# A decay product in bf16 over three exact terms, with dummy products ahead of the heads, in an three-phase gated block on one core

## What is computed

```python
def _mlstm_head(q, k, v, ig, fg, eps=1e-06):
    log_f = jax.nn.log_sigmoid(fg)
    cs = jnp.concatenate([zeros, jnp.cumsum(log_f, axis=0)], axis=0)
    log_d = jnp.where(jnp.tri(s, dtype=bool), (cs - cs.T)[1:, 1:] + ig.T, neg)
    m = jnp.max(log_d, axis=-1, keepdims=True)
    d = jnp.exp(log_d - m)
    c = q @ (k.T / jnp.sqrt(dh)) * d
    n = jnp.maximum(jnp.sum(c, axis=-1, keepdims=True), jnp.exp(-m))
    return c / (n + eps) @ v
...
gate_in = jnp.concatenate((q, k, v), axis=-1)      # q = layernorm(x), k = v = ctx
ig = gate_in @ igate_kernel + igate_bias
fg = gate_in @ fgate_kernel + fgate_bias
```

## Time and profile before

| | us |
|---|---|
| runs | 608.34, 601.44, 603.51; median 603.51 |
| profiled execution: time | 601.67 |
| profiled execution: span from first to last instruction | 599.9 |
| TensorE busy | 474.9 (79%) |
| VectorE busy | 346.9 (58%) |
| ScalarE busy | 306.2 (51%) |
| GpSimd busy | 237.9 (40%) |
| granted TensorE clock, mean | 0.859 |

### The profile page before, as it was taken

One profiled execution on the slowest core, in us unless ns is written; L12 is line 12 of the kernel. 1 busy time (PEld: TensorE's weight loads), 2 busy tenths in 40 slices (PEclk: granted clock), 3 DMA queues, 4 the chain that ended last, 5 costly groups with the idle time before them and its releaser, 6 DMA issues. The chain is left out here.

```text
span 599.9 us, 12767 instructions
## 1 busy us (share of the span) xinstructions
PE 474.9 (79%) x3771; PEld 352.3 (59%) x3771; DVE 346.9 (58%) x1447; ACT 306.2 (51%) x764; POOL 237.9 (40%) x226
## 2 busy tenths in 40 slices
PE   0349999999999999974459999999607777777774
PEld 0337677877787778663327777777504445455552
DVE  6223588687878777787312333332214787788873
ACT  1346576666666656422113333333215677777873
POOL 5200114444444444466500000000088888888810
PEclk9998788677777767895569999999955999999998
DMA  5981112222222211140122343333143556555521
GB/s 139 184 162 55 54 55 75 70 68 75 67 76 68 73 52 50 43 124 27 36 62 54 105 106 105 105 106 89 52 101 45 111 120 136 120 108 128 134 72 52
DMA packets 85067, 51.98 MB, mean 87 GB/s; under 512 B 7555, under 2 KB 78886, under 8 KB 85030
## 3 DMA queue, kind: packets, MB, share of 16 engines
q1 hardware_dynamic: 73766, 43.09, 27.0%
q0 software_dynamic: 11264, 8.43, 8.2%
HBM read 26.07 MB, written 16.91 MB: 72 GB/s over the span
## 5 line engine op out<-in xcount | busy, mean ns | idle before, releaser
L665 POOL DMA_INDIRECT s_xs<-slots_y,s_gidx x64 | 98.9, 1545 | 152.3 <-DMA slots_y<-s_ye 134.7
L803 ACT ACTIVATE s_ht<-heads,s_cols 128x512 f32<-128x512 f32 x64 | 44.0, 687 | 85.1 <-PE heads L1044 84.8
L147 ACT ACTIVATE s_xn<-s_xs,s_ln_shift,s_ln_rstd 128x128 f32 (+1 forms) x192 | 77.6, 481 | 17.2 <-DVE s_ln_shift L140 16.8
L99 DVE BATCH_NORM_STATS2 s_ln_stats<-s_xs 128x6 f32 (+1 forms) x256 | 55.0, 280 | 35.2 <-DMA s_xs<-slots_y,s_gidx 19.2
L643 POOL DMA_INDIRECT slots_x<-s_xn,s_sidx x64 | 62.8, 982 | 22.9 <-issue 22.9
L629 POOL TENSOR_TENSOR s_hs<-s_hs,s_head_w 128x512 f32<-128x512 f32 x16 | 20.3, 1268 | 109.0 <-DVE s_hs L1268 108.9
L1044 PE MATMUL heads<-s_xet,s_w_sb 128*128 128x512 f32 x128 | 59.8, 612 | 1.7 <-DVE s_xet L1384 1.7
L1051 PE MATMUL bank<-s_w_sb,s_ht 128*128 128x128 f32 x512 | 59.9, 276 | 0.9 <-DVE s_ye L1393 0.9
L1051 PEld LDWEIGHTS bank<-s_w_sb,s_ht 128*128 128x128 f32 x512 | 58.5, 192 | 1.5 <-issue 1.5
L943 PE MATMUL heads<-s_dec_r,s_dec_l 128*128 128x512 f32 x64 | 50.6, 938 | 0.0
L968 PE MATMUL heads<-s_vaug,s_cw 64*64 64x33 f32 x1024 | 47.4, 261 | 0.3 <-DVE s_cw L1230 0.3
(11 more groups left out here) (181 smaller groups left out, 962.0 us busy)
## 6 DMA issues: line engine op xcount, KB each, us to landing
slots_x<-s_xe SPq DMA_DIRECT2D x8, 516.0 KB, 11.4
s_xe<-slots_x SPq DMA_DIRECT2D x16, 258.0 KB, 3.2
s_xs<-in_x_dram SPq DMA_DIRECT2D x16, 256.0 KB, 2.9
s_ctxb<-in_ctx_dram SPq DMA_DIRECT2D x16, 256.0 KB, 3.1
s_kpt<-s_kt SPq DMA_DIRECT2D x16, 256.0 KB, 2.4
s_w_sb<-in_L_ffn_w_dram SPq DMA_DIRECT2D x16, 256.0 KB
slots_y<-s_ye SPq DMA_DIRECT2D x16, 256.0 KB, 2.3
s_ctxv<-in_ctx_dram SPq DMA_DIRECT2D x16, 256.0 KB
```

Of the source, the lines that this page charges most:

```text
L99: last = dve.bn_stats(self.stats[:, i * GT + t, :], tile(t))
L147: last = act.activation(out(t), tile(t), ACT.Identity, bias=self.shift[:, j:j + 1], scale=self.rstd[:, j:j + 1])
L665: pool.indirect_dma_start(out=xs[:, n * D:(n + 1) * D], out_offset=None, in_=slots_y, in_offset=bass.IndirectOffsetOnAxis(ap=gidx[:, n:n + ...
L803: act.activation(ht[:, s_par, c, :], heads[:, c, :], ACT.Gelu_apprx_tanh, bias=col).then_inc(h_done, 1)
```

## The change

An fp32 value is split into three terms. Its upper half-word, read as bf16, is the first term; what is left after subtracting it is an fp32 value again, whose upper half-word is the second term, and once more for the third. The three sum to the value. `top_half` reads every second half-word of an fp32 tile as bf16, so that no term is written as bf16 anywhere.

`am` gets 48 columns (three groups of 16) and `mrow` three rows of 128 for each pair. VectorE computes the differences: two more steps after `am` and two after the scan, each waiting for the one before. `turn_a` transposes 48 columns, the copy to `dec_l` takes 48 rows, six DMAs in place of two bring the maxima to rows 48 to 53 of `dec_r`, and SP's two waits ahead of them change places. The two products of `decay_exponents` read the upper halves of both operands. On GpSimd the constants are written for the new rows (`CONSTS` 30 to 34). And TensorE's `first_pass` calls `keep_clock(1, 4)` after `gate_products`: four dummy products of 512 columns to bank 1.

```diff
+def top_half(ap):
+    return ap.bitcast(BF16).rearrange("p (n w) -> p n w", w=2)[:, :, 1]
...
-        am = sb("am", [P, 2, R])
-        mrow = sb("mrow", [R, 2, P])
+        am = sb("am", [P, 2, 3 * R])
+        mrow = sb("mrow", [R, 2, 3, P])
+        pick = sb("pick", [3 * R, 2, R])
...
             def spread_max(g, half, q):
+                hold(sp, l_ps, g - 1, consts)
                 hold(sp, mrow_done, g + 1, consts)
-                hold(sp, l_ps, g - 1, consts)
-                for b in range(2):
-                    sp.dma_start(dec_r[32 + b:33 + b, q, :], mrow[:, q, b * S:(b + 1) * S]).then_inc(m_in[q], 16)
+                for j in range(3):
+                    if j:
+                        hold(sp, m_terms, nth(g, j, 2), consts)
+                    for b in range(2):
+                        row = 3 * R + 3 * b + j
+                        sp.dma_start(dec_r[row:row + 1, q, :], mrow[:, q, j, b * S:(b + 1) * S]).then_inc(m_in[q], 16)
...
             def turn_a(g, half, q):
-                pe.wait_ge(a_done, g + 1)
-                pe.transpose(bank[6][0:R, 128:256], am[:, q, :], ident[:, :]).then_inc(at_ps, 1)
+                hold(pe, a_terms, nth(g, 2, 2), consts)
+                pe.transpose(bank[6][0:3 * R, 128:256], am[:, q, :], ident[:, :]).then_inc(at_ps, 1)
...
             def decay_exponents(g, half, q):
                 pe.wait_ge(arow_done, g + 1)
-                hold(pe, m_in[q], half * 32 + 32, consts)
+                hold(pe, m_in[q], half * 96 + 96, consts)
                 need(pe, cw_done, nth(g - 1, 2, 2))
                 for u in range(2):
-                    last = pe.matmul(heads[:, u, :], dec_l[:, q, :], dec_r[:, q, u * GW:(u + 1) * GW], start=True, stop=True)
+                    last = pe.matmul(heads[:, u, :], top_half(dec_l[:, q, :]), top_half(dec_r[:, q, u * GW:(u + 1) * GW]),
+                                     start=True, stop=True)
...
                 if one:
                     gate_products(*one)
+                    keep_clock(1, 4)
                 if three:
                     head_values(*three)
...
             def a_values(g, half, q):
-                dve.tensor_tensor(am[:, q, :], gates[:, 0, :], bank[6][:, 64:64 + R], ALU.subtract).then_inc(a_done, 1)
+                dve.tensor_tensor(am[:, q, 0:R], gates[:, 0, :], bank[6][:, 64:64 + R], ALU.subtract).then_inc(a_done, 1)
+                dve.wait_ge(a_done, g + 1)
+                for j in range(2):
+                    if j:
+                        dve.wait_ge(a_terms, nth(g, 1, 2))
+                    term = am[:, q, j * R:(j + 1) * R]
+                    dve.tensor_tensor(am[:, q, (j + 1) * R:(j + 2) * R], term, top_half(term), ALU.subtract).then_inc(a_terms, 1)
...
             def running_max(g, half, q):
-                dve.tensor_copy(dec_l[0:R, q, :], bank[6][0:R, 128:256]).then_inc(arow_done, 1)
+                dve.tensor_copy(dec_l[0:3 * R, q, :], bank[6][0:3 * R, 128:256]).then_inc(arow_done, 1)
...
-                dve.tensor_tensor_scan(mrow[:, q, :], reset[:, :], bank[6][0:R, 128:256], 0.0, ALU.add, ALU.max).then_inc(mrow_done, 1)
+                dve.tensor_tensor_scan(mrow[:, q, 0, :], reset[:, :], bank[6][0:R, 128:256], 0.0, ALU.add, ALU.max).then_inc(mrow_done, 1)
+                dve.wait_ge(mrow_done, g + 1)
+                for j in range(2):
+                    if j:
+                        dve.wait_ge(m_terms, nth(g, 1, 2))
+                    term = mrow[:, q, j, :]
+                    dve.tensor_tensor(mrow[:, q, j + 1, :], term, top_half(term), ALU.subtract).then_inc(m_terms, 1)
```

More of the change, by code:

```diff
@@ L338, in flamingo @@
         a_done = sem("a_done")
+        a_terms = sem("a_terms")
+        m_terms = sem("m_terms")
         at_ps = sem("at_ps")
@@ L429, in one_row @@
             return v.rearrange("(a n) -> a n", a=1)
-        CONSTS = 30
+        CONSTS = 34
         block = ctx.enter_context(nc.Block())
@@ L598, in _ @@
             pool.wait_ge(cleared, 4)
[L599 to L602, removed]
+            step(pool.memset(pick[:, :, :], 0.0))
+            for j in range(3):
+                step(pool.affine_select(out=pick[:, :, :], in_=pick[:, :, :], compare_op=ALU.not_equal, fill=1.0, base=-j * R,
+                                        pattern=[[0, 2], [-1, R]], channel_multiplier=1))
+            step(pool.tensor_copy(dec_r[0:3 * R, :, :].rearrange("p q (r i) -> p (q r) i", i=S),
+                                  pick[:, :, :].rearrange("p q r -> p (q r)").unsqueeze(2).to_broadcast([3 * R, 2 * R, S])))
             step(pool.tensor_copy(dec_r[S:P, :, :].rearrange("p q (r i) -> p (q r) i", i=S),
@@ L606, in _ @@
                                   ident[S:P, S:P].unsqueeze(1).to_broadcast([S, 4, S])))
[L607 to L611, removed]
+            step(pool.memset(dec_l[32:S, :, :], -1.0))
+            for b in range(2):
+                half = dec_l[32:S, :, b * S:(b + 1) * S]
+                step(pool.affine_select(out=half, in_=half, compare_op=ALU.is_ge, fill=0.0, base=32 - 3 * R - 3 * b,
+                                        pattern=[[0, 2], [0, S]], channel_multiplier=1))
+                step(pool.affine_select(out=half, in_=half, compare_op=ALU.is_ge, fill=0.0, base=3 * R + 3 * b + 2 - 32,
+                                        pattern=[[0, 2], [0, S]], channel_multiplier=-1))
             step(pool.memset(reset[:, :], 0.0))
@@ L1219, in running_max @@
                 need(dve, l_ps, g - 1)
-                dve.tensor_copy(dec_l[0:R, q, :], bank[6][0:R, 128:256]).then_inc(arow_done, 1)
+                dve.tensor_copy(dec_l[0:3 * R, q, :], bank[6][0:3 * R, 128:256]).then_inc(arow_done, 1)
                 if not isinstance(g, int) or g >= 2:
-                    dve.wait_ge(m_in[q], half * 32)
-                dve.tensor_tensor_scan(mrow[:, q, :], reset[:, :], bank[6][0:R, 128:256], 0.0, ALU.add, ALU.max).then_inc(mrow_done, 1)
+                    dve.wait_ge(m_in[q], half * 96)
+                dve.tensor_tensor_scan(mrow[:, q, 0, :], reset[:, :], bank[6][0:R, 128:256], 0.0, ALU.add, ALU.max).then_inc(mrow_done, 1)
[5 more added lines that the diff above has]
+                    dve.tensor_tensor(mrow[:, q, j + 1, :], term, top_half(term), ALU.subtract).then_inc(m_terms, 1)
             def decayed_scores(g, q, u):
```

2 lines of the change are left out of this document (1 added, 1 removed).

## The result

| | before | after |
|---|---|---|
| median of the runs, us | 604.46 (601.44 to 608.34, 4 runs) | 620.07 (617.61 to 629.66, 4 runs) |
| ratio, 95% interval | | 1.0241 [1.0149, 1.0333] |
| profiled execution, time and span, us | 601.67, 599.9 | 617.61, 615.9 |
| granted clock over the span | 0.859 | 0.805 |

The time is inside the range of the prediction (591 to 628), but not where its forecast put it (606, within 1% of before). What came is the first rival, the clock that comes back only with the scores, for which the prediction gave 0.30 and 625 us. The interval of the ratio is clear of 1, but not of 2%.

What follows compares the result with a forecast made beforehand. The first phase was taken as bound by a loop through VectorE and TensorE, with TensorE's clock; -1.0, +1.0 and +0.35 us a pass made +4.6 over 13 passes, less 2 at the ends: 606 us, range 591 to 628.

Steps and rivals of the forecast that it cites:

- the first rival: TensorE's clock comes back only with the scores: 2.4 us a pass in 9 of 13, 625 us, chance 0.30.
- stretch A: From `s_am` to the one-hot in each pass, 4.30 us, taken to belong to VectorE.
- stretch B: From the one-hot to the next `s_am`, 10.41 us, taken to belong to TensorE, with VectorE waiting 1.59 us at its end.
- (1): Decay product on TensorE as two bf16 products: 0.60 us high, about 1.0 low, saving 2.3 a pass.
- (2): Four dummies ahead of the heads on TensorE: 0.86 us high, 1.7 low, 1.3 in the mean, on the path.
- (3): Four more VectorE steps between `s_am` and the one-hot: 0.42 and 0.62 us, taken as +1.0 a pass.
- (4): `turn_a` on TensorE waits for the second term and turns 48 columns instead of 16: nothing, at most 0.1 us.
- (5): Six row transfers on SP instead of two: 3.5 us of issue, hidden with 2.6 us to spare.
- (6): GpSimd's setup changes by four steps, swallowed by VectorE's later 6.78 us wait for a transfer of `s_xs`: 0.
- The late terms: Rival: the decay product waits for the sixth row, half a microsecond late, +0.5 a pass, 612 us, chance 0.07.
- (7): TensorE's clock stays low over turns and logits in about one pass of three: +0.35 us a pass.
- the ends of the phase: Three first passes and one last of the first phase, where B alone counts: 4 x -0.5 = -2 us.

Runs made afterwards that it cites:

- e2: The kernel before with only the four dummy products added between gates and heads: 626.16 us, ratio 1.0338 to the kernel before.
- e10: The changed kernel with only the first term and 17 dummies spread over the pass in place of four: 587.26 us, ratio 0.9727 to the kernel before.
- e9: The changed kernel with all three terms and 17 dummies spread over the pass in place of four: 595.26 us, ratio 0.9862 to the kernel before.
- e7: The kernel before with only the four VectorE steps added, their results unused: 625.47 us, ratio 1.0218 to the kernel before.
- e6: The changed kernel without dummies and with only the first term, so no added VectorE steps: 604.66 us beside 606.61 of the kernel before.
- e1: The changed kernel without its four dummy products: 612.04 us, ratio 1.0109 to the kernel before.
- e4: The changed kernel with 13 dummies spread over token count, gates and heads in place of four: 604.32 us, ratio 0.9920 to the kernel before.
- e5: The kernel before, with fp32 product and no added VectorE steps, given 13 spread dummies: 610.92 us beside 606.61 of the kernel before.
- e8: The changed kernel with 13 spread dummies and the two `s_mrow` steps on GpSimd instead of VectorE: 630.27 us, ratio 1.0340 to the kernel before.

## Why the prediction was right in its range and wrong in its forecast

The frame held: one loop, stretch A with VectorE, stretch B with TensorE, and the clock over both. Of the seven steps:

- **(1) The product**: right. 1.06 us low and 0.61 high for the two, taken as 1.0 and 0.60. The strided operands cost nothing that shows, so the upper bound of 1.88 is out.
- **(2) The dummies**: the size was off. 1.3 us was a mean of both levels, the runs show 1.55 a group in after and 1.75 in e2, since the level falls just there. "Net of (1) and (2) on B: -1.0" would have been -0.6.
- **(3) The four steps**: their length was right (0.38 and 0.59 against 0.42 and 0.62; A grew from 4.5 to 5.3 in the mean from the 7th to the 14th pass, and by 1.0 from e10 to e9). By the formula of the Trainium skill (VectorE: DVE Perf Modes, section on the TRN2 errata) one such `s_mrow` step is estimated at 0.29 us, and the trace has 0.59 for two. Wrong was that they cost just their length. In the long passes of after they are hidden: the one-hot is done at 169.3 us and TensorE's scores at 170.8, and TensorE waits for the one-hot for 1.0 us in all of the steady part. In e7, with the fp32 product, they cost 1.7 a pass. The step took A and B as separate terms, and what a longer A costs depends on when TensorE comes to the one-hot, and at which level it goes on.
- **(4), (5), (6)**: right. L959 is in no pass behind `s_dec_r`; its idle time is 0.2 us of its own issue. Six issues took 3.79 us (3.5 predicted), landing 1.8. The late terms are out. On setup, the wait of the earlier trace rows became 5.56 us at 37.76, 1.4 us sooner.
- **(7) The clock**: this is the step that failed. It took +0.35 a pass, the low level over turns and logits in one pass of three. Measured per group are +0.79 on the turns, +0.52 on the logits, +0.91 on the scores and +0.58 on the heads, 2.8 together. With the product (-2.1), the dummies (+1.55) and the gates (-0.25) this is +2.0 of busy time, which overlaps at its edges, for passes 1.5 longer. Scores ran low in 9 of 16 groups, and the first rival had "9 of 13" passes at 2.4 us; what happened is 7 of ten steady passes at 2.3 over the mean of before (17.30 less 15.04), and three between 0.7 under it and 0.6 over.

Some of the agreement is luck. For the ends of the phase the sum had -2, at half of B's -1.0 a pass and without a reason for the half. The two end stretches gave -3.4 and +1.4. Two readings were off without harm: A from +0.6 to +1.3 and a clock term from 0 to +0.6 would span 596 to 613, not 599 to 612, and issues of 0.9 us would bring the last row 0.3 us late, not 0.5.

Terms (2), (3) and (7) failed in one way. Each was priced on levels and waits that I took as given from before, and the change moves them. The sum of +0.35 a pass was the clock term alone, with bounds of -0.4 and +2.1, so its sign was undecided, and the evidence for the upper side was already in the trace: the level was back for the logits behind L943 in every steady pass, and the change takes two thirds of L943 away. That this matters is shown by e6, where the product alone is changed.

The Trainium skill (TensorE: Matmul & The Clock Gate, section PE-mode transpose) says that transposes don't count as busy for the clock in the way that other products do; by that rule the rival was what happens. The traces agree in the seven long passes, where the low level lasts through eight turns (1.10 and 1.06 us) and ends in the scores. They do not prove it: in other passes of after the level came back earlier, with scores at 1.95, and no run here set transposes against plain products in the same place.

## What to carry to other kernels

Where the granted clock moves within a loop, a stage's time is not its own: price the whole loop at each level, and ask of a shortened product whether the clock used to come back behind it. Four dummies in one place bought nothing here (e1, e2, after), while 17 of them spread over the whole sparse stretch held the clock (1.00 in e9), and they pay only if something else then is faster than they are long. Try a change of several parts one part at a time: here the dummies alone (3.4%) and the steps alone (2.2%) each cost about as much as all three parts together (2.4%), or more.

## What the runs showed that I had not expected

- Dummies alone made the kernel before 3.4% slower, and 17 spread ones with the short product made it 1.4% faster.
- Behind TensorE pauses of 0.7 to 1.0 us ahead of the one-hot's count the gates ran wholly or in part at 1.2 GHz in nine of ten passes (e7: 320 ns a record for 275).
- What the level is worth differs by stage: a gate product takes 0.37 us high and 0.57 low, the 32 head products (64 records) 2.06 and 3.63, the 8 score products (16 records) 1.95 and 3.68.
- Two `s_mrow` steps took 0.59 us on VectorE and 0.92 on GpSimd. The kernel with them on GpSimd was 4% slower than e4, for a reason that is open: they were not late, and the clock was low for 20 us and more at a time.
- What is still open: why the level, once lost in e4, e5 and e8, stays low for passes of 18 to 26 us in spite of 13 dummies, and what part the transposes have in its return. Neither was tried by itself.
